# A recommendation tower's lookups on one core: squares kept in PSUM, twenty fields by one-hot matmul instead of eighteen

## What is computed

```python
e = stack([tbl_f[ids[:, f]] for f in range(39)], axis=1)     # [B, 39, 64]
delta = einsum('uf,bfe->bue', inner_w, e)                    # [B, 128, 64]
z = sum(delta * delta, axis=-1)                              # [B, 128]
h = concatenate([z, dense_ctx], axis=1)                      # [B, 144]
h = maximum(h @ W_top1 + b_top1, 0)                          # 512
h = maximum(h @ W_top2 + b_top2, 0)                          # 256
y = h @ W_top3                                               # [B, 1]
```

## Time and profile before

| | us |
|---|---|
| median of 3 runs | 570.38 |
| the runs | 564.09, 572.16, 570.38 |
| the profiled execution | 569.8 |
| its span, first to last instruction | 568.1 |
| TensorE busy (matmul) | 445.9 (78%) |
| TensorE busy (weight load) | 388.9 (68%) |
| VectorE busy | 440.6 (78%) |
| GpSimd busy | 412.0 (73%) |
| ScalarE busy | 224.3 (39%) |
| granted TensorE clock, mean | 0.916 |

### The profile page before, as it was taken

One profiled execution on the slowest core, in us unless ns is written; L12 is line 12 of the kernel. 1 busy time (PEld: TensorE's weight loads), 2 busy tenths in 40 slices (PEclk: granted clock), 3 DMA queues, 4 the chain that ended last, 5 costly groups with the idle time before them and its releaser, 6 DMA issues.

```text
span 568.1 us, 10177 instructions
## 1 busy us (share of the span) xinstructions
PE 445.9 (78%) x3376; PEld 388.9 (68%) x3376; DVE 440.6 (78%) x716; ACT 224.3 (39%) x312; POOL 412.0 (73%) x343
## 2 busy tenths in 40 slices
PE   0556869887799769968999879967998799865566
PEld 0556858786688659857878668856987698744334
DVE  2899759898689967868988967868989998854631
ACT  2543124243244433423533433443544444443432
POOL 6888778778777778778887878778887887872000
PEclk9997999899899888988999889988999999966677
DMA  6773477667776666748776666747766886474510
GB/s 174 211 198 88 116 213 228 201 176 191 187 210 191 192 165 172 212 111 222 207 197 188 192 177 177 211 123 223 213 203 171 227 218 187 129 214 123 183 50 1
DMA packets 67594, 100.43 MB, mean 177 GB/s; under 512 B 15750, under 2 KB 22554, under 8 KB 67548
## 3 DMA queue, kind: packets, MB, share of 16 engines
q1 hardware_dynamic: 56696, 88.61, 52.1%
q0 software_dynamic: 10752, 11.03, 10.3%
q10 hardware_dynamic: 100, 0.16, 0.1%
HBM read 36.31 MB, written 0.16 MB: 64 GB/s over the span
## 4 chain that ended last, share of the span: by engine, by line
POOL 72%; issue 19%; PE 4%; DMA 2%; SPq 1%; ACT 1%; DVE 1%; POOLq 0%; ACTq 0%
POOL x_all L389 72%; PE side L456 2%; PE side L448 1%; SPq L338 1%; PE delta L489 1%; DMA xs<-xl 1%; ACT sq_all L557 1%; DMA x_all<-tbl,idx 0%; DMA dense_f<-dense_t 0%; PE side L461 0%; PE turned L475 0%; DVE z L668 0%; DMA idx<-ids 0%; SPq L347 0%; ACT h L566 0%
## 5 line engine op out<-in xcount | busy, mean ns | idle before, releaser
L389 POOL DMA_INDIRECT x_all<-tbl,idx x336 | 411.3, 1224 | 103.6 <-issue 101.8
L431 PE MATMUL side<-table,onehot 125*128 125x192 bf16 x2496 | 245.2, 259 | 43.8 <-DVE table L718 19.1
L431 PEld LDWEIGHTS side<-table,onehot 125*128 125x128 bf16 x2496 | 218.1, 104 | 68.7 <-issue 48.8
L489 PE MATMUL delta<-xs,ws 117*128 117x512 f32 (+1 forms) x272 | 121.8, 488 | 63.2 <-DMA xs<-xl 48.5
L664 DVE TENSOR_TENSOR acc_all<-acc_all,sq_all 128x1024 f32<-128x1024 f32 x112 | 136.5, 1219 | 18.3 <-ACT sq_all L557 17.3
L541 ACT ACTIVATE xh<-turned 117x512 fp32r<-117x512 f32 x96 | 54.0, 562 | 208.4 <-PE turned L475 201.2
L637 DVE TENSOR_SCALAR onehot<-idh,row_no 125x1024 bf16<-125x1024 f16 x312 | 130.1, 481 | 6.9 <-DMA idh<-ids 6.9
L656 DVE TENSOR_REDUCE x_all<-side 128x128 f32<-128x384 f32 x144 | 77.0, 551 | 64.2 <-PE side L431 63.2
L557 ACT ACTIVATE sq_all<-delta 128x1024 f32<-128x1024 f32 x112 | 112.4, 1022 | 28.9 <-PE delta L489 27.9
L489 PEld LDWEIGHTS delta<-xs,ws 117*128 117x128 f32 x272 | 52.4, 211 | 82.6 <-DMA xs<-xl 41.5
L475 PEld LDWEIGHTS turned<-ident,x_all 128*117 128x117 f32 x352 | 86.3, 310 | 9.3 <-DMA x_all<-tbl,idx 6.1
(11 more groups left out here) (30 smaller groups left out, 80.5 us busy)
## 6 DMA issues: line engine op xcount, KB each, us to landing
xs<-xh SPq DMA_DIRECT2D x160, 234.0 KB
xs<-xl SPq DMA_DIRECT2D x80, 234.0 KB
idh<-ids SPq DMA_DIRECT2D x72, 224.0 KB
x_all<-tbl,idx POOLq DMA_INDIRECT x336
xs<-xh SPq DMA_DIRECT2D x32, 117.0 KB
x_all<-tbl SPq DMA_DIRECT2D x12, 224.0 KB
idh<-ids SPq DMA_DIRECT2D x72, 26.0 KB
xs<-xl SPq DMA_DIRECT2D x16, 117.0 KB
```

What stands on the lines that cost most here:

```text
L389: pool.indirect_dma_start(x_slots[k][:, f, 0:E], None, tables[f], bass.IndirectOffsetOnAxis(idx[k][:, f:f + 1], 0),).then_inc(gathered[k], 16)
L431: mm = pe.matmul(side[n % 2][:, q * PARTS * E:(q + 1) * PARTS * E], onehot[k % OHR][:, c, q, h * TB:(h + 1) * TB], table[k][:, q, c, :, :] ...
L489: mm = pe.matmul(delta[quad % 2][:, c:c + cols], ws[:, :], xs[i % XS][:, j, 0:SIZE[u], :].rearrange("p g b -> p (g b)"), start=True, stop= ...
```

## The change

1. The tile `sq` goes. ScalarE writes the squares of quads 1 to 7 back into the delta buffer that they were read from, in PSUM. VectorE adds that buffer to acc. A project now waits for the add of the quad two before; where that is quad 0, whose square goes to acc, for the square.
2. A tenth pair of ten chunks: 20 fields by lookup, 19 gathered. The lookup jobs have new due times, a pair every two units, and the mlp jobs lie between them.
3. `onehot` stays at three buffers, and `idh` has two instead of three. The ids' staging tiles at the start lie in acc instead of sq.

```diff
-PAIR_CH = [8] * 6 + [10] * 3
+PAIR_CH = [8] * 6 + [10] * 4
...
-SQ = 2
 OHR = 3
...
-IDR = 3
+IDR = 2
...
 JOBS = [
-    ("look", (0, 0), -0.9), ("look", (0, 1), -0.5), ("look", (1, 0), 1.4), ("look", (1, 1), 1.9),
-    ("mlp", 0, 3), ("look", (2, 0), 3.8), ("look", (2, 1), 4.3), ("look", (3, 0), 6), ("look", (3, 1), 6.5),
-    ("mlp", 1, 7.2), ("look", (4, 0), 8.4), ("look", (4, 1), 8.9), ("mlp", 2, 10), ("look", (5, 0), 10.6),
-    ("look", (5, 1), 11.1), ("mlp", 3, 11.8), ("look", (6, 0), 12.8), ("look", (6, 1), 13.3),
-    ("look", (7, 0), 15), ("look", (7, 1), 15.5), ("look", (8, 0), 17.2), ("look", (8, 1), 17.7),
+    ("look", (0, 0), -0.9), ("look", (0, 1), -0.4), ("look", (1, 0), 1.1), ("look", (1, 1), 1.6),
+    ("look", (2, 0), 3.1), ("look", (2, 1), 3.6), ("mlp", 0, 3.9), ("look", (3, 0), 5.1),
+    ("look", (3, 1), 5.6), ("look", (4, 0), 7.1), ("look", (4, 1), 7.6), ("mlp", 1, 7.9),
+    ("look", (5, 0), 9.1), ("look", (5, 1), 9.6), ("mlp", 2, 10.6), ("look", (6, 0), 11.1),
+    ("look", (6, 1), 11.6), ("mlp", 3, 12.5), ("look", (7, 0), 13.1), ("look", (7, 1), 13.6),
+    ("look", (8, 0), 15.1), ("look", (8, 1), 15.6), ("look", (9, 0), 17.1), ("look", (9, 1), 17.6),
 ]
...
-        sq_all = sb("sq_all", [P, SQ, 4 * NB], F32)
-        sq = [sq_all[:, k, :] for k in range(SQ)]
...
@@ project (TensorE)
-                    if n % 2 == 0:
-                        wait(pe, squared, at_quads(s, h) + quad - 1)
+                    if n % 2 == 0 and quad == 2:
+                        pe.wait_ge(squared, at_quads(s, h) + 1)
+                    elif n % 2 == 0:
+                        wait(pe, summed, at_sums(s, h) + quad - (2 if quad > 2 else 1))
...
@@ square (ScalarE)
-                    if quad == 0:
-
-                        to = acc[h]
-                    else:
-                        wait(act, summed, at_sums(s, h) + quad - 1 - (SQ - 1))
-                        to = sq[(h * (QUADS - 1) + quad - 1) % SQ]
+                    to = acc[h] if quad == 0 else delta[quad % 2]
...
@@ add (VectorE)
-                    dve.tensor_tensor(acc[h][:, :], acc[h][:, :], sq[(h * (QUADS - 1) + quad - 1) % SQ][:, :], ALU.add).then_inc(summed, 1)
+                    dve.tensor_tensor(acc[h][:, :], acc[h][:, :], delta[quad % 2][:, :], ALU.add).then_inc(summed, 1)
```

More of the change, by code:

```diff
@@ L169, in build @@
         ident = sb("ident", [P, P], F32)
-        sq_all = sb("sq_all", [P, SQ, 4 * NB], F32)
-        sq = [sq_all[:, k, :] for k in range(SQ)]
-        ids_all = sq_all[0:PAIRS * STEPS, 0, 0:2 * NB].bitcast(I32)
-        ids_low = sq_all[0:PAIRS * STEPS, 1, 0:DUP * NB].bitcast(F16).rearrange("p (d c) -> p d c", d=DUP)
         acc_all = sb("acc_all", [P, 2, 4 * NB], F32)
+        ids_all = acc_all[0:PAIRS * STEPS, 0, 0:2 * NB].bitcast(I32)
+        ids_low = acc_all[0:PAIRS * STEPS, 1, 0:DUP * NB].bitcast(F16).rearrange("p (d c) -> p d c", d=DUP)
         acc = [acc_all[:, k, :] for k in range(2)]
```

## The result

The changed kernel takes 634.97 us (median of 4 runs, 634.85 to 640.98) against 568.92 us for the kernel before: a ratio of 1.1216, 95% interval 1.1118 to 1.1314. It is 12% slower, where 563 us and a range of 543 to 590 were forecast. The profiled execution took 640.98 us, and its times are used here.

The account below looks back on a forecast made before the run. GpSimd's gathers were taken to bound it through SyncE's queue. Pace 56.6 + 3.6 + 1.7 - 1.4 = 60.5 us; 112 + 6 x 60.5 = 475, then 475 + 48 + 38.3 + 1.7 = 563.0 us, range 543 to 590.

Parts of the forecast that it names:

- What bounds the kernel now: Whole kernel before: GpSimd's gathers set the pace through a DMA queue, 61.8 us a superstep.
- the lock on SP's queue: SyncE's reload of idx stops for gathers once a superstep, holding restacks behind it; costs 5 to 6 us a superstep.
- own pace: TensorE's and VectorE's superstep time without SyncE's stop for gathers: 56.6 us, each 90% busy.
- Rival 4: SyncE's stop did not make 61.8 us; look-ups simply add: 65.4 us a superstep, 592 us; chance 0.08.
- Part 1, gathers: GpSimd: 38 gathers a superstep instead of 42, no longer stretched by adds: 49.7 us in place of 62.
- Rival 5: GpSimd's gathers stay 1.49 us apart despite the changed add; SyncE's stop returns in places: pace 61, 566 us; chance 0.05.
- Part 2, look-ups: TensorE: the tenth pair's 40 matmuls add 3.6 us a superstep, mostly on the path; bounds 0.3 and 3.6.
- Part 3, VectorE: VectorE: one more one-hot and two fills, +3.1 us a superstep beside the look-ups; add and square times unchanged.
- Part 4, squares in PSUM: Projects wait for the add of the quad two before: 1.7 us a superstep, bounds 0 and 5.4.
- gone into restack waits: TensorE: 1.4 us of added look-ups and later delta reuse absorbed by 3.3 us of restack waits a superstep.
- Rival 3: Delta reuse becomes the bound, TensorE waiting for VectorE's adds: 64.2 us a superstep, 585 us; chance 0.17.
- Part 5, start and queues: Start: extra pair 5.8 us, first z at 112; SP's ten one-hot waits a superstep instead of nine cost 0.

Follow-up runs that it names:

- idx_late_b: The kernel before with SP's reload of idx moved from 1.5 to 8 units in its order: 571.62 us, ratio 1.003 to the kernel before.
- sbuf20_b: The changed kernel with squares back in SBUF, twenty fields, three xh and xl slots instead of four, narrower idx: 590.66 us, ratio 1.0362 to the kernel before.

## Why the prediction was wrong, by its own steps

**What bounds the kernel now.** Right in its mechanism: the lock on SP's queue was there (idx_late_b), it went with the change, and GpSimd's rate was the true bound. The own pace was read from one superstep, 56.6 us at a clock of 1.00, and that one was not typical; two supersteps without the lock take 58.6 at 0.97. That is 2.0 us of the miss. Rival 4 (the lock was not what made 61.8) falls.

**Part 1, gathers.** Right. A gather beside the changed add is as short as alone:

```profile
189.12 1.22 DVE L659 TENSOR_TENSOR acc_all<-acc_all,delta 128x1024 f32<-128x1024 f32 x1 [3.57 <-ACT delta L552]
...
189.81 0.94 POOL L387 DMA_INDIRECT x_all<-tbl,idx  x1 [0.30 <-issue]
```

against the 2.32 us of the earlier trace rows. (That one is a long case: it starts while a one-hot still runs, and the add follows.) The mean is 1056 ns in the changed kernel, 1059 with squares in PSUM alone and 1233 with twenty fields and squares in SBUF, so it goes with the squares' place and not with the number of fields. Two things moved with that place, the add's operand and what ScalarE writes, and the traces tell them apart. Of the gathers with no one-hot beside them, 58 start inside an add in the kernel before. 43 of these are stretched, up to 2.03 us, and end 0.8 us after the add. The 47 that were already running when an add started take 0.94 or 0.95. In the changed kernel 57 start inside an add, and each takes 0.94 or 0.95. In the kernel before 46 gathers overlap a square and neither add nor one-hot, and they too take 0.94 or 0.95. So it is the add with both operands in SBUF.

The Trainium skill (SBUF — State Buffer, "Who interferes with whom") infers that such an add spares descriptor generation. An indirect DMA is not spared here, by 165 to 177 ns in the mean. Whether it is descriptor generation that is held up or the gather's reading of idx, no run here tells, so the inference is not borne out for a gather as a whole and stays open for descriptor generation alone. Rival 5 falls with it. The gain was real and bought nothing, as GpSimd was no longer late for anything.

**Part 2, look-ups.** The 40 matmuls were priced well (busy time of TensorE from 52.8 us a superstep in idx_late_b to 56.7 in the same two supersteps of sbuf20_b, 3.9 against 3.6). The step that failed is the overlap: 58.6 to 64.7 is 6.1 us, where 3.6 less a share of 1.4 was booked. Idle time did not soak up the new work but grew by some 2 us, from 5.8 to 8.0. SP's stops for one-hots grow beside it: 60.5/6 = 10 us a superstep in sbuf20_b, and 8.8 us in two in idx_late_b. Whether those stops (two idh buffers), the new order, VectorE's 3.1 us or the three slots make it was not settled.

**Part 3, VectorE.** Right: the add with a PSUM operand takes 1213 ns against 1219, the square into PSUM 1014 against 1022. The 65 ns more that were estimated from the Trainium skill (VectorE: DVE Perf Modes, "The TRN2 errata") for a PSUM source do not show.

**Part 4, squares in PSUM.** This is the step that failed most, a term of the sum that was taken too small, and the choice in it was mine. The count over the trace gave 5.4 us a superstep of late reuses; I took 1.7 and let 1.4 of this and of part 2 go into restack waits. In the first two supersteps the runs show 63.3 against 58.6 with eighteen fields, 4.7 us, and 71.2 against 64.7 with twenty, 6.5 (5.7 over six). In the start and the end it costs as well (z of step 0 at 119.4 against 112.1, the end 41.2 against 37.2), which the sum had at nothing.

The terms of the sum, in us a superstep, beside what the runs show over the first two:

| term | forecast | measured |
|---|---|---|
| own pace, eighteen fields | 56.6 | 58.6 |
| tenth pair | 3.6 | 6.1 |
| squares in PSUM | 1.7 | 6.5 |
| gone into restack waits | -1.4 | in the two above |
| sum | 60.5 | 71.2 |

The miss of 10.7 us is 2.0 of own pace, 2.5 of look-ups, 4.8 of squares in PSUM and 1.4 of absorption. The last did take place, 12.6 us of restack waits and 9.1 of waits for fills in six supersteps, but the new waits were 45.0 us, 7.5 a superstep, well above the count.

That the count of 5.4 comes near the net price is in part luck. It is an average that has the start and the end in it; from z of step 0 to z of step 6 it is 4.2. And made in the same way over the trace of sbuf20_b, whose order is the changed kernel's, it gives 59 late reuses there and 8.5 us a superstep. Rival 3 named this mechanism and its place, VectorE's queue, and came out at 64.2, since it started from 56.6, had 3.6 for the look-ups and let 1.4 be absorbed. ScalarE's queue in front of the square was part of no case; moving its copies as well gave another 13 us.

**Part 5, start and queues.** The extra pair's 5.8 us at the start were right (112.1 in sbuf20_b). "SP ten times instead of nine: 0" is open: these waits went from 50.9 to 91.9 us, and what they cost was not isolated.

## What to carry to other kernels

Before a buffer between two engines is lent to a third, count from the old trace how many of its reuses would come too late, in the order that the new kernel will have, and book the sum rather than a third of it. Idle time elsewhere did take up half of the new waits here, and the supersteps still grew by as much as the whole count, since the delayed engine also makes what the others wait for. Two buffers shared by three in-order queues live on the order in these queues; move the holders' work (here adds ahead of one-hots, squares ahead of copies not yet due) before judging the design. A pace read from one superstep should be checked against another. And an engine that fills the chain of waits can be the bound and still be worth little, when the next ones are 90% busy.

## What the runs showed of the hardware that was not expected

An indirect DMA on GpSimd that starts inside a VectorE add with both operands in SBUF is held up (43 of 58, up to 2.03 us against 0.94), one that starts inside an add with an operand in PSUM is not (none of 57), and one that was already running is not either (none of 47). And the time of one program can change from set to set: it takes 569 or 770 us, by stretches in which TensorE gets an instruction only every 1.4 us and a gap of 23.8 us, and a variant that is 3% slower in the one case is 18% slower in the other.
